# Moving VectorE's weighted sums of expert outputs behind the last groups of a mixture-of-experts stage

## The reference, cut to what matters

```
x = x + tanh(g_xattn[0]) * attention_0(layernorm(x), ctx)
# feed-forward of layer 0: 8 experts, each token takes 2, plus a shared one
logits  = layernorm(x) @ gate_w.T ;  top 2 of softmax, rescaled to sum 1 -> combine
y       = gelu(layernorm(x) @ W1[e] + b1[e]) @ W2[e] + b2[e]        # per expert e
x = x + tanh(g_ffn[0]) * (combine[token, e1]*y[token, e1] + combine[token, e2]*y[token, e2] + shared)
# layer 1
x = x + tanh(g_xattn[1]) * attention_1(layernorm(x), ctx)
```

## Time and profile before

| what | value |
|---|---|
| three timed runs | 1071.5, 1072.06, 1078.28 us; median 1072.06 |
| the profiled execution, own time | 1074.33 us |
| its span, first to last instruction | 1071.5 us |
| mean granted TensorE clock | 0.949 of full speed |
| TensorE busy (matmul) | 919.6 us, 86% |
| VectorE busy | 736.7 us, 69% |
| ScalarE busy | 661.0 us, 62% |
| GpSimd busy | 621.2 us, 58% |
| expert stage of layer 0 | VectorE's outputs (L1380) start from 279.7 to 441.65 us |

### The profile page before, as it was taken

How to read it: one execution, slowest core, us unless ns; L and a number is a source line. 1 busy time by engine, 2 the same in 40 slices (tenths; PEclk the granted TensorE clock), 3 DMA queues, 4 the chain that set the end, 5 groups by cost and what they waited for, 6 DMA issues and landing times. The chain is left out here.

```text
span 1071.5 us, 22118 instructions
## 1 busy us (share of the span) xinstructions
PE 919.6 (86%) x7691; PEld 746.2 (70%) x7691; DVE 736.7 (69%) x1613; ACT 661.0 (62%) x1581; POOL 621.2 (58%) x697
## 2 busy tenths in 40 slices
PE   2799999896978996787799999999999988648995
PEld 1576777674978986655577676777777666438995
DVE  6799995553447675679999895555555568736774
ACT  2677777432644654587688886666666556436884
POOL 0477775456564154588878676444444466632675
PEclk9799999998998998899999999999999999858998
DMA  8970000012331332010000000000500000020311
GB/s 241 321 229 2 2 1 2 1 37 68 94 89 41 89 97 63 23 36 22 20 2 2 2 2 1 1 2 2 152 26 2 1 2 1 24 76 22 103 52 40
DMA packets 62288, 53.30 MB, mean 50 GB/s; under 512 B 7491, under 2 KB 54979, under 8 KB 61988
## 3 DMA queue, kind: packets, MB, share of 16 engines
q1 hardware_dynamic: 55588, 38.33, 12.3%
q0 software_dynamic: 6592, 13.58, 4.1%
HBM read 33.14 MB, written 21.99 MB: 51 GB/s over the span
## 5 line engine op out<-in xcount | busy, mean ns | idle before, releaser
L2213 POOL TENSOR_TENSOR ring<-ring,mx 128x1024 f32<-128x1024 f32 x85 | 162.3, 1915 | 101.1 <-DVE mx L2089 100.9
L1965 ACT ACTIVATE pT<-psT 128x512 f32<-128x512 f32 x192 | 114.5, 597 | 124.3 <-PE psT L1815 124.3
L1278 ACT ACTIVATE pT<-psS,b1copy 128x128 f32<-128x128 f32 x468 | 133.5, 369 | 84.2 <-PE psS L1221 84.1
L1221 PE MATMUL psS<-ring 128*128 128x128 f32 x936 | 133.9, 290 | 21.9 <-DVE ring L1346 19.9
L1815 PE MATMUL psT<-ident,ring 128*128 128x128 f32 x768 | 124.2, 285 | 19.8 <-ACT pT L1965 9.1
L1221 PEld LDWEIGHTS psS<-ring 128*128 128x128 f32 x936 | 123.1, 205 | 24.4 <-DVE ring L1346 21.8
L1815 PEld LDWEIGHTS psT<-ident,ring 128*128 128x128 f32 x768 | 85.8, 143 | 67.1 <-issue 36.0
L2081 DVE TENSOR_TENSOR ring<-psS,bias 128x1024 f32<-128x1024 f32 x96 | 112.6, 1215 | 9.8 <-PE psS L1804 8.1
L2089 DVE TENSOR_REDUCE mx<-ring 128x16 f32<-128x1024 f32 x96 | 112.2, 1209 | 0.0
L1449 POOL DMA_INDIRECT xrows<-sorted_y,rows x64 | 67.3, 1051 | 68.8 <-DMA sorted_y<-pT 34.7
L1343 DVE COPY ring<-w 128x512 f32 x117 | 53.6, 458 | 70.3 <-PE psO L1231 49.7
(11 more groups left out here) (323 smaller groups left out, 2167.5 us busy)
## 6 DMA issues: line engine op xcount, KB each, us to landing
w<-w_dram SPq DMA_DIRECT2D x34, 256.0 KB, 6.0
sorted_x<-late SPq DMA_DIRECT2D x18, 256.0 KB, 3.4
ring<-sorted_x SPq DMA_DIRECT2D x18, 256.0 KB
sorted_y<-pT SPq DMA_DIRECT2D x17, 256.0 KB
sorted_z<-blank_dram SPq DMA_DIRECT2D x2, 1584.0 KB, 10.1
x<-sorted_z SPq DMA_DIRECT2D x5, 264.0 KB, 4.3
xnT<-sorted_z SPq DMA_DIRECT2D x5, 264.0 KB, 4.6
ctxz<-ctxz_dram SPq DMA_DIRECT2D x1, 1056.0 KB, 5.5
```

The lines of the kernel that those rows point to most:

```text
L1221: mm = nc.tensor.matmul(psS[:, j % 2, f * P:(f + 1) * P], wcopy[:, j % 4, 0, f, :], xgT[:, s, t * P:(t + 1) * P], start=True, stop=True)
L1278: op = nc.scalar.activation(hs[:, j % 2, f, :], psS[:, j % 2, f * P:(f + 1) * P], func, bias=b1copy[:, j % 4, f:f + 1])
L1965: nc.scalar.activation(pT[:, u % 2, 4 * h:4 * h + 4, :].rearrange("p a q -> p (a q)"), psT[:, :], ACT.Exp).then_inc(s_pT, 1)
L2213: nc.gpsimd.tensor_tensor(rows_, rows_, mx[:, u % 4, 0:NH].rearrange("p h -> p h ()").broadcast_to([P, NH, SK]), ALU.subtract).then_inc(s_ ...
```

## The change

Five edits, all in the order of the instructions; the computation is the same.
- The combine of chunk 0, with the gates ahead of it, stands ahead of the copies of group 15 and no longer of group 13.
- The combine of chunk 1 stands ahead of the outputs of group 17, behind that group's place for copies, and no longer in group 14.
- The combines of chunks 2 and 3 stand behind the outputs of the last group, and no longer in groups 15 and 16.
- GpSimd makes the norm factors of chunk 0 alone, between the gathers of chunk 1 and those of chunk 2, and waits there for the statistics of chunk 0. Those of chunks 1 to 3 it makes where it made all four.
- ScalarE waits for s_first of 1 for chunk 0 and of 2 for the chunks 1 to 3.

```diff
@@ moe_vector @@
-            m = n - (1 if r == 0 else 0) - NC // 2
             for g in range(n):
-                if r == 0 and m <= g < m + NC // 2:
-                    if g == m:
-                        gates_vector(dve)
-                    combine(dve, 0, 0, g - m)
+                if r == 0 and g == COMBINE_AT[0]:
+                    gates_vector(dve)
+                    combine(dve, 0, 0, 0)
...
+                if r == 0 and g == COMBINE_AT[1]:
+                    combine(dve, 0, 0, 1)
                 outputs(g)
+            if r == 0:
+                for c in range(2, NC // 2):
+                    combine(dve, 0, 0, c)
+
+        COMBINE_AT = (GROUPS[0] - 3, GROUPS[0] - 1)
+
+        def first_deviations(pool, chunks):
+
+            pool.wait_ge(s_bn1, CH * chunks[-1] + CH)
+            k = slice(chunks[0], chunks[-1] + 1)
+            deviations(pool, st[:].rearrange("p (c t) s -> p c t s", c=NC)[:, k], lna0[:, k], lnd0[:, k], lnr0[:, k], lnb0[:, k], lnh0[:, k], s_first)
@@ fetch_half @@
             for cc in chunks:
                 fetch(pool, r, h * (NC // 2) + cc, range(CH * CHOICES[r]))
+                if cc == 1:
+                    first_deviations(pool, range(0, 1))
@@ stream_scalar, normalise @@
-                    act.wait_ge(s_first, 1)
+                    act.wait_ge(s_first, 2 if c else 1)
@@ stream_gpsimd @@
             pool.wait_ge(s_four, FOUR_SET)
-            pool.wait_ge(s_bn1, CH * (NC // 2))
-            deviations(pool, st[:].rearrange("p (c t) s -> p c t s", c=NC)[:, 0:NC // 2], lna0[:], lnd0[:], lnr0[:], lnb0[:], lnh0[:], s_first)
+            first_deviations(pool, range(1, NC // 2))
```

## The result

The changed kernel takes 1076.88 us (median of 20 runs, 1073.13 to 1081.34), the kernel before, beside it, 1073.25 (20 runs, 1069.35 to 1078.28). The ratio is 1.0039 with an interval of 1.0027 to 1.0051: 4.2 us slower, 2.9 to 5.5, and under 1%. The profiled execution has a span of 1074.9 us against 1071.5.

What follows compares the result with a forecast made beforehand. TensorE, the busiest engine, idles 19.9 us for VectorE's weight copies; the stage ends 14.1 to 14.9 us earlier, but the stream starts +2.0 later, chosen between +0.2 and +4.35: 1072.06 becomes 1074.1 us, range 1067 to 1080.

Steps and rivals of the forecast that it cites:

- Copies freed: VectorE, groups 13, 14 and 16: outputs 13 at 393.33, outputs 14 at 401.96, 3.86 us earlier than before.
- gates and chunk 0 ahead of group 15: VectorE: group 15 takes 11.44 us, outputs 15 at 413.40, outputs 16 at 420.98, chunk 0's statistics end at 406.98.
- chunk 1 ahead of outputs 17: VectorE: 3.37 us within 5.86 us of idle, cost nothing; at most 3.4 if that cover were gone.
- GpSimd waits in the middle of its gathers: GpSimd waits for chunk 0's statistics until 407.1; first gather of chunk 2 at 410.2, 13 us later than before.
- The four bursts: GpSimd's gathers of chunks 2 and 3 take 27.4 us, so chunk 3 lands at 437.6 (435.6 to 444.2).
- What hangs on chunk 3: Combine until 441.0, factors until 445.9, chunk 1 normed at 447.55, scores 1 at 451.2: first turning of probabilities +1.45 us.
- The clock: TensorE after its pause: turning, values and scores 1 take 2.9 us more at 1.2 GHz, +4.35 in sum; warm, +1.45.
- The stream behind has no other slack: Stream behind its first steps: a shift at its start, taken as +2.0 us, reaches the end whole.
- A: Rival: GpSimd gets to chunks 2 and 3 in time, 1067.5 us; with factors hidden too 1064.3; chance 0.13.
- B: Rival: GpSimd's subtractions and the second half's gathers bind the stream's first steps, 1072.3 us; chance 0.20.
- C: Rival: all four bursts land slowly, 34.0 us, and the restart is cold, 1083 us; chance 0.07.
- D: Rival: chunk 0's factors come late, ScalarE stalls at tile 67, stage's end isn't earlier, 1074 us; chance 0.03.

Runs made afterwards that it cites:

- second group: Runs on one chip, kernel before 1120.8 us: changed kernel again 1.0119; changed kernel with chunk 0's factors made after chunk 2's gathers 1.0031.
- first group: Runs on one chip, kernel before 1108.65 us; among them the changed kernel with gates and combine of chunk 0 in group 16, not 15: 1127.01 us, 1.0157.
- chunks 0 and 1 as before: Changed kernel with gates and combine of chunk 0 back in group 13, chunk 1 in group 14: 1069.03 us, 0.9956 to the kernel before.
- second trace of the kernel before: Kernel before, unchanged, profiled again as a run of its own: 1073.09 us, ratio 1.0000.
- spread version: Changed kernel with gates, chunks 0, 1 ahead of groups 13, 14, 15, chunk 2 ahead of outputs 17; factors of 0 and 1 after chunk 2's gathers: 1063.78 us, 0.9917.
- third measurement: Later runs on one chip, kernel before 1072.86 us, each compared with it; the changed kernel itself was not among them.
- the kernel with the factors after chunk 2: Changed kernel with GpSimd making chunk 0's factors after chunk 2's gathers: 1127.25 us, 1.0031; earlier, on another chip, 1115.86 us, 1.0061.

## Why the prediction was right, point by point

The forecast (the tail hangs on chunk 3's gathers, nothing that can be measured at 1%) held, and 1076.88 us lies in the range; the size was under-estimated, +4.2 us by the ratio (3.6 by the medians) and not +2.0.

- *Copies freed; gates and chunk 0 ahead of group 15; chunk 1 ahead of outputs 17*: 7.58, 8.44 and 11.36 us for the groups 13 to 15, against 7.58, 8.63 and 11.44. Group 17 took 5.50, a little under the taken 5.8 to 6.55. Net, outputs 17 are 15.5 us earlier; 14.1 to 14.9 were expected.
- *GpSimd waits in the middle of its gathers*: it started again at 405.72 (predicted 407.1, 406.0 net), and the first gather of chunk 2 came at 409.65 (410.2, 409.1 net). The power for 4 values took 1.29 us, where the earlier trace rows had 1.02. Moved behind 8 of the gathers this wait costs 0.88% less (second group), moved one group later it costs more (first group), and where it is free the kernel beats the one before (chunks 0 and 1 as before): shown.
- *The four bursts*: 27.3 us from 409.65 to 436.94, 27.4 taken. One of the four was again longer than the others, 7.64 us.
- *What hangs on chunk 3*: factors were made from 440.31 to 444.59, 4.3 us with 4.95 taken; chunk 1 normed in 1.65 us as in the earlier trace rows, until 446.28 (447.55, 446.49 net). So at ScalarE the chain was met within 0.2 us net, by terms that were up to 0.7 us off and cancel.
- *The clock* is the term that was mis-sized for the first turning. The three pieces took 1.11 + 2.07 + 2.00 = 5.18 us against 2.91 before, 2.27 more, where the upper end had 2.9 for it and the 2.0 taken left 0.55. With +1.45, and 0.35 less in all from the terms ahead and the hand-over behind, that gives 3.37, the net delay of the first turning (2.31 plain). The section of the Trainium skill that the prediction named, "HAM oscillation — how this bites in real kernels" in "TensorE: Matmul & The Clock Gate", has such a piece start cold after its wait. The trace agrees behind the pause of 18.48 us, with 0.51 in the window from 446.30, but not for every pause: the second trace of the kernel before has matmuls at the full clock behind 2.04 and 1.95 us. The prediction's sentence that the restarts of the earlier trace rows bear the rule out rests on one execution.
- *"The stream behind has no other slack"* was wrong. Scores 2 start at 456.75, where the two traces of the kernel before have 456.85 and 455.50: the first of these had its own stretch at 1.2 GHz there, the second not, so the delay of the first turning is down to nothing or 1.25 us. Scores 4 start at 473.99 against 472.57 and 472.94, behind a VectorE subtraction that took 4.75 us and not 1.22 (next section); this term was not in my sum, and that it brought part of the delay back was not tried alone. The last scores start at 919.64 against 917.82 and 917.64, 1.8 to 2.0 us later. The two traces of the kernel before are 1.08 us apart at the first turning and 0.18 at the last scores: a shift at the start doesn't reach the end whole. That 1.8 to 2.0 is also the +2.0 of the forecast is luck, since it came by other terms. The spans differ by 3.4 and 2.6 us, so another 0.6 to 1.6 arises behind the last scores; whether that and the rest up to 4.2 is the change or the spread of executions stays open.

Of the rivals: A (gathers don't gate) fell by the 8.20 us wait. The version in which the wait is free, chunks 0 and 1 as before, took 1069.03 us where A had 1067.5; that the spread version's 1063.8 meets A's best, 1064.3, is luck, as its stage ends 4 us before the 427.4 that A goes by. B (GpSimd sets the pace) fell: GpSimd's first subtraction started at 447.98, net 449.04, as its bound had it (448.9), but the next steps waited for others: VectorE 5.31 us for TensorE's scores 1 (452.21), and GpSimd 0.85 us for VectorE's maxima (456.96). C (over 1%) fell, as the bursts took 27.3 us and not 34. D (first factors late) fell: ScalarE normed chunk 0 at 417.88 with no wait. The mechanism of the prediction, the place of GpSimd's wait, was the right one. Two smaller points: group 13's excess of 3.86 us, half of it put down to a cold restart, holds for the one trace (2.3 in the other), and the +2.0 was a choice between bounds and not a sum.

## What to carry to other kernels

A wait put into an in-order queue is paid by everything behind it: here the norm factors of one chunk ahead of 16 gathers turned a stage that ends 15.5 to 16.6 us sooner into a start that is 2.3 to 3.4 us later. Place each piece where its length fits the slack of its group: gates and combine of 5.0 us together left TensorE idle for about 2 us, a combine of 3.1 alone for 0.96, and behind the keys of layer 1 for none. Then follow the chain that is left once a wait has gone, first on the queue and then on the engines: with the combines of chunks 2 and 3 behind the last group it took 13 us from the last outputs to the next turning, and 2.6 before. And before a low clock in one trace goes into a sum, look at a second trace of the same kernel.

## What the runs showed of the hardware that I had not expected

**A subtraction that takes four times as long.** VectorE's subtraction of two arrays of 128x1024 in on-chip memory took 1.22 us in the kernel before and 4.75 in the changed one. VectorE's timeline of the kernel before:

```profile
463.87 1.22 DVE L2094 TENSOR_TENSOR ring<-ring,mx 128x1024 f32<-128x1024 f32 x1
```

GpSimd's, of the same kernel:

```profile
465.92 1.28 POOL L2227 TENSOR_TENSOR x<-x,bx 128x512 f32<-128x512 f32 x1
```

And GpSimd in the changed kernel, beside the 464.06 row above:

```profile
464.59 1.27 POOL L2240 TENSOR_TENSOR x<-x,bx 128x512 f32<-128x512 f32 x1
465.83 1.89 POOL L2226 TENSOR_TENSOR ring<-ring,mx 128x1024 f32<-128x1024 f32 x1
```

GpSimd's two instructions take their usual 1.27 and 1.89 us and cover 464.59 to 467.72; VectorE has 4.75 - 1.22 = 3.53 us more, about their 3.16. In the version with chunks 0 and 1 as before the same row took 4.30 us, in the spread version, where GpSimd's addition came 2 us behind its end, 1.22. It goes the other way too. VectorE's timeline of the kernel before:

```profile
448.48 1.22 DVE L2094 TENSOR_TENSOR ring<-ring,mx 128x1024 f32<-128x1024 f32 x1
```

This one took its 1.22 us, and GpSimd's subtraction, which started at 448.64, took 2.81 and not 1.90. The Trainium skill, "SBUF — State Buffer", section "SBUF: two separate sides", says that a VectorE operation with two inputs in SBUF and a GpSimd operation that reads SBUF share a pair of ports, which the one that starts first holds for a whole instruction while the other stands. The traces agree that one of the two stands, and at 448.48 with the order; at 464.06 VectorE's record starts 0.53 us ahead of GpSimd's and yet it is VectorE that loses the time.

**Chips differ.** The kernel before took 1073.25 and 1072.86 us in the first and third measurement and 1108.65 and 1120.8 on two other chips. The traces there show stalls of ScalarE and VectorE that are put down to "remote", none of which stand in the traces of the first and the third. One instance, ScalarE's timeline in the second group, in the kernel with the factors after chunk 2:

```profile
384.13 1.14 ACT L1278 ACTIVATE pT<-psS,b1copy 128x128 f32<-128x128 f32 x4 [2.36 <-remote]
```

What these are stays open. Differences of a few us are therefore safe only within one group; those to the changed kernel in the third group go by ratios from two measurements. What such stalls cover or uncover in the experts' stage was not settled, since the kernel before was not profiled on those chips.
